# A mixture-of-experts tail: where the third shared-expert batch is computed

## The chip, the cores and the metric

The kernel runs on one NeuronCore of a Trainium2 chip. The metric is the device time of one launch in microseconds (us). TensorE is called PE, VectorE DVE, ScalarE ACT, GpSimd POOL and SyncE SP, as the profile does.

## What is computed

Four batches of 512 tokens, each token a row of 256 numbers, go through two layers, all in float32:

```python
x = x + xattn(layernorm(x), ctx)              # 16 heads, causal mask
xf = layernorm(x).reshape(2048, 256)
comb = top-2 softmax weights over 8 experts, from xf @ gate_w.T
for e in range(8):                            # HALF = 384
    y = silu(xf @ wg[e].T) * (xf @ wu[e].T) @ w_down[e].T
    out += comb[:, e:e+1] * y
shared = silu(xf @ sg_gate.T) * (xf @ sg_up.T) @ sg_down.T
x = x + shared + out
```

The change touches only the second layer: the shared expert, which every token passes, and its place beside the eight routed experts.

## The kernel before

**Order.** Every engine has its own instruction list, written out by hand, and the lists meet at semaphores. There is no planner; what stands first on an engine's list runs first. After attention come the second layernorm, the router (a chain of small DVE instructions), the lists of tokens by expert (`token_of`, semaphore `lists_ready`), and then 39 expert tiles of 128 token slots each (`NT` = 39).

**Shared expert.** It runs by batch `b` of 512 tokens, B = 4 batches, with M = 3 pieces `m` of the hidden width. `shared_up(b)` on PE makes gate and up values of a piece in PSUM `set_a`; `shared_silu(b, m)` on ACT and `shared_h(b, m)` on DVE turn them into `sg[:, m]`; `shared_down(b)` on PE multiplies by the down weights into `set_b`, banks 2 and 3; `shared_y(b)` on DVE adds that to the residual rows `x_res`. The last batch is added by two instructions of its own at the very end (L1596). `s_h` counts the `shared_h` that are done, `s_yfree` the batches whose down result has left PSUM (it starts at 1). In the kernel before, batches 0, 1 and 2 run before the expert tiles, in the time of the router and the weight splits, and batch 3 runs after them.

**Weight splits.** The expert up-weights (`wup`) are split into a high and a low part in 8 pieces (`SPLITS`): ACT copies a piece to `wup_hi` (`hi_parts`, L986), DVE writes `wup_lo` = `wup` - `wup_hi` (`lo_part`, L1478). `up_lo` counts the finished low pieces; PE waits for all 8 before the first expert tile. The first four high pieces (`EARLY` = 4) are made before the lists are known.

**Expert tiles.** POOL gathers the rows of a tile from DRAM (`rows_in_tile`, L576). PE transposes them (`rows_t`, L901), ACT and DVE split the result (L986, L1505), PE runs `up` (12 matmuls, L914 to L916), ACT and DVE make the hidden values, PE transposes these (L924) and runs `down` (L933 to L935), DVE weights the result (L1531), and POOL adds the rows to one of two sums in DRAM with an indirect DMA (`add_rows`, L584). The tiles are software pipelined, one tile to a slot.

**End.** When all tiles of a sum are added, SP loads the sum back by four DMAs of 512 tokens (L455, first sum 1, then sum 0), DVE adds them to `x_res` (`add_sum`, L1583; four adds of 128x1024 for sum 1, eight of 128x512 for sum 0), and ACT's queue stores each eighth of `x_res` (L1200). In the kernel before, `shared_h(3, m)` stands on DVE's list in turn with the adds of sum 1.

Of the kernel before, what the change touches and what calls it, by code (L numbers as in the profile page):

```python
# [41 lines left out]
DMA = 16  # L42


def build(nc, x, ctxT, wqT, bq, wkT, bk, wvT, bv, woT, bo, gwT, wupT, wdnT, sgT, suT, sdT, out):
    B, S, D = x.shape
# [6 lines left out]
    QT = S // P  # L53
# [4 lines left out]
    M = HALF // P  # L58
    TOP_K = 2
    NT = (TOP_K * N + E * (P - 1)) // P  # L60
# [19 lines left out]
    with ExitStack() as ctx:  # L80
# [3 lines left out]
        def sem(name):  # L84
            return ctx.enter_context(nc.semaphore(name))
# [129 lines left out]
        def te():  # L215
# [56 lines left out]
        s_up, s_sg, s_h, s_y, s_yfree = (sem(n) for n in ("s_up", "s_sg", "s_h", "s_y", "s_yfree"))  # L272
# [5 lines left out]
        y_in = [[sem(f"y_in{i}_{c}") for c in range(B)] for i in range(2)]  # L278
# [3 lines left out]
        e_xt, e_xTr, e_up, e_sgr, e_hr, e_ht, e_hTr, e_yf, e_yr = (sem(n) for n in  # L282
            ("e_xt", "e_xTr", "e_up", "e_sgr", "e_hr", "e_ht", "e_hTr", "e_yf", "e_yr"))
# [59 lines left out]
        SPLITS = 8  # L343
        EARLY = 4

        def piece(w, i):
            cut = C * E * 2 * HALF // SPLITS
            return w[:].rearrange("p c n -> p (c n)")[:, i * cut:(i + 1) * cut]
# [250 lines left out]
        def _(pe):  # L599
# [235 lines left out]
            def shared_up(b, lo=0, hi=M):  # L835
                for m in range(lo, hi):
                    n = b * M + m
                    if n > 1:
                        pe.wait_ge(s_h, n - 1)
                    for w, dst in zip((wsg, wsu), gu[n % 2]):  # L840
                        for c in range(C):
                            last = mm(dst, w[:, c, m * P:(m + 1) * P], xn2T[:, c, bass.ds(b * S, S)],  # L842
                                      start=c == 0, stop=c == C - 1)
                    last.then_inc(s_up, 1)

            def shared_down(b):
                pe.wait_ge(s_yfree, b + 1)
                for m in range(M):
                    pe.wait_ge(s_h, b * M + m + 1)
                    for j in range(QT):  # L850

                        last = mm(Bk[:, 2 + j // 2, (j % 2) * D:(j % 2 + 1) * D], sg[:, m, j * P:(j + 1) * P],  # L852
                                  wsd[:, m, :], start=m == 0 and j % 2 == 0, stop=m == M - 1,
                                  skip_group_check=True)
                last.then_inc(s_y, 1)
# [34 lines left out]
                          at_tile[:, j, :, :].rearrange("p c t -> p (c t)"), start=j == 0, stop=j == NJ - 1)  # L890
            last.then_inc(hot_full, 1)
            shared_down(1)
            shared_up(2, 0, 2)


            def rows_t(t, a, x, filled, first=False):
                pe.wait_ge(e_in[x], DMA * filled)
                if not first:
                    pe.wait_ge(e_xTr, t)
                for c in range(C):  # L900
                    last = tr(Bk[:, 0, c * P:(c + 1) * P], e_x[:, x, c * P:(c + 1) * P], ident[:])  # L901
                last.then_inc(e_xt, 1)
# [4 lines left out]
            def up(t, a, e):  # L907
                pe.wait_ge(e_xTr, t + 1)
                for i in range(2):
                    for c in range(C):  # L910
                        cols = bass.ds(e * (2 * HALF) + i * HALF, HALF)
                        dst = A[:, 2 * a + i, 0:HALF]

                        mm(dst, e_xT_hi[:, a, c, :], wup_hi[:, c, cols], start=c == 0, stop=False)  # L914
                        mm(dst, e_xT_hi[:, a, c, :], wup_lo[:, c, cols], start=False, stop=False)  # L915
                        last = mm(dst, e_xT_lo[:, a, c, :], wup_hi[:, c, cols], start=False, stop=c == C - 1)  # L916
                last.then_inc(e_up, 1)

            def hidden_t(t, a, first=False):
                pe.wait_ge(e_hr, t + 1)  # L920
                if not first:
                    pe.wait_ge(e_hTr, t)
                for m in range(M):
                    last = tr(Bk[:, 1, m * P:(m + 1) * P], e_h[:, a, m * P:(m + 1) * P], ident[:])  # L924
                last.then_inc(e_ht, 1)

            def down(t, a, e):
                pe.wait_ge(e_hTr, t + 1)
                pe.wait_ge(e_yr, t + 1)
                cols = bass.ds(e * D, D)  # L930
                dst = Bk[:, 2, 0:D]
                for m in range(M):
                    mm(dst, e_hT_hi[:, a, m, :], wdn_hi[:, m, cols], start=m == 0, stop=False)  # L933
                    mm(dst, e_hT_hi[:, a, m, :], wdn_lo[:, m, cols], start=False, stop=False)  # L934
                    last = mm(dst, e_hT_lo[:, a, m, :], wdn_hi[:, m, cols], start=False, stop=m == M - 1)  # L935
                last.then_inc(e_yf, 1)
# [1 line left out]

            pe.wait_ge(hot_read, 1)
            rows_t(0, 0, 0, 1, True)  # L940
            shared_up(2, 2, 3)
            rows_t(1, 1, 1, 1)
            shared_down(2)
            pe.wait_ge(experts_known, 1)
            first = [expert(t) for t in range(3)]
            pe.wait_ge(up_lo, SPLITS)
            pe.wait_ge(s_h, (B - 1) * M)
            up(0, 0, first[0])
            rows_t(2, 0, 2, 1)
            up(1, 1, first[1])  # L950
            rows_t(3, 1, 3, 1)
            pe.wait_ge(s_yfree, B)
            hidden_t(0, 0, True)
            up(2, 0, first[2])

# [21 lines left out]
            down(NT - 2, (NT - 2) % 2, e_last[1])  # L977
            down(NT - 1, (NT - 1) % 2, e_last[2])
            pe.wait_ge(e_hr, NT)
            shared_up(3)  # L980
            pe.wait_ge(e_yr, NT + 1)
            shared_down(3)

        @block.scalar
        def _(act):
# [147 lines left out]
            def shared_silu(b, m):  # L1133
                act.wait_ge(s_up, b * M + m + 1)
                nc.scalar.activation(sg[:, m, :], gate[(b * M + m) % 2], ACT.Silu).then_inc(s_sg, 1)

            def hi_parts(pieces):
                for i in pieces:
                    copy(piece(wup_hi, i), piece(wup, i)).then_inc(up_hi, 1)
# [6 lines left out]
                shared_silu(1, m)  # L1146
            act.wait_ge(lists_ready, 1)
            act.wait_ge(who_stored, DMA)
            hi_parts(range(EARLY, EARLY + 1))
            shared_silu(2, 0)  # L1150
            hi_parts(range(EARLY + 1, EARLY + 2))
            shared_silu(2, 1)
            hi_parts(range(EARLY + 2, SPLITS))

            def rows_t(t, a):
                act.wait_ge(e_xt, t + 1)
                copy(e_xT_hi[:, a], Bk[:, 0, 0:C * P].rearrange("p (c n) -> p c n", c=C)
                     ).then_inc(e_xhi, 1)
# [7 lines left out]
                copy(e_hT_hi[:, a], Bk[:, 1, 0:M * P].rearrange("p (c n) -> p c n", c=M)).then_inc(e_hThi, 1)  # L1166

            rows_t(0, 0)
            shared_silu(2, 2)
            rows_t(1, 1)  # L1170
            silu(0, 0)
            rows_t(2, 0)
# [15 lines left out]
            silu(NT - 1, (NT - 1) % 2)  # L1188
            hidden_t(NT - 2, (NT - 2) % 2)
            hidden_t(NT - 1, (NT - 1) % 2)  # L1190
            for m in range(M):
                shared_silu(3, m)
            o_t = out.rearrange("b (k p) d -> p (b k) d", p=P)
            for c in range(2 * B):
                if c // 2 < B - 1:
# [7 lines left out]
        def _(dve):  # L1203
# [188 lines left out]
            def shared_h(b, m):  # L1392
                dve.wait_ge(s_sg, b * M + m + 1)
                up_ = (A[:, 1, :], A[:, 3, :])[(b * M + m) % 2]
                v.tensor_tensor(sg[:, m, :], up_, sg[:, m, :], ALU.mult).then_inc(s_h, 1)

            def shared_y(b):
                dve.wait_ge(s_y, b + 1)
                rows = xs_all[:, bass.ds(b * QT, QT), :]
                v.tensor_tensor(rows, Bk[:, 2:4, :].rearrange("p a (k d) -> p (a k) d", k=2), rows,  # L1400
                                ALU.add).then_inc(s_yfree, 1)
# [74 lines left out]
            def lo_part(i):  # L1476
                dve.wait_ge(up_hi, i + 1)
                v.tensor_tensor(piece(wup_lo, i), piece(wup, i), piece(wup_hi, i), ALU.subtract).then_inc(up_lo, 1)  # L1478
# [13 lines left out]
            v.tensor_reduce(tok, lists, AX.X, ALU.add).then_inc(hot_read, 1)  # L1492
            dve.wait_ge(hot_read, 1)
            v.tensor_scalar(token_of[:], tok, io_np, None, ALU.add).then_inc(lists_ready, 1)  # L1494
            shared_y(1)

            lo_part(2)
            shared_h(2, 0)
            lo_part(3)
            lo_part(EARLY)  # L1500
            shared_h(2, 1)

            def rows_lo(t, a):
                dve.wait_ge(e_xhi, t + 1)
# [33 lines left out]
            lo_part(EARLY + 1)  # L1538
            rows_lo(0, 0)
            lo_part(EARLY + 2)  # L1540
            shared_h(2, 2)
            rows_lo(1, 1)
            lo_part(EARLY + 3)
            weights(0, 0, True)
            weights(1, 1, True)
            shared_y(2)
            hidden(0, 0)
            rows_lo(2, 0)
            weights(2, 2)
# [31 lines left out]
            def add_sum(i, at, ready):  # L1581
                dve.wait_ge(*ready)
                v.tensor_tensor(xs_all[:, at, :], xs_all[:, at, :], y_sum[i][:, at, :], ALU.add).then_inc(y_added, 1)  # L1583

            for m in range(M):
                shared_h(3, m)
                add_sum(1, slice(m * QT, (m + 1) * QT), (y_in[1][m], DMA))
            add_sum(1, slice(T - QT, T), (y_in[1][B - 1], DMA))
            for c in range(2 * B):
                dve.wait_ge(y_added, c // 2 + 1)  # L1590
                add_sum(0, slice(2 * c, 2 * c + 2), (y_in[0][c // 2], DMA))
# [43 lines left out]
```

## Time and profile before

| what | value |
|---|---|
| median of 3 runs | 506.07 us (505.5 to 507.34) |
| the profiled execution's own time | 505.84 us |
| its span in the profile | 504.1 us |
| mean granted TensorE clock | 0.977 |
| PE busy | 455.0 us, 90% |
| DVE, ACT, POOL busy | 309.2, 210.1, 193.2 us |
| HBM traffic | 81 GB/s over the span |

The span runs from the first to the last instruction of the profiled execution; its own time is 1.74 us longer. A busy PE is not a PE at its peak, since the ends of matmuls are modelled. Busy shares are averages over stages that are limited by different things, so the rows further down are taken stage by stage. The granted clock is a share of 2.4 GHz; 0.5 is the lower level, 1.2 GHz.

### The profile page before, as it was taken

To read this page: it belongs to the slowest core of one execution; us is meant where nothing else is said; L and a number is where in the kernel's file an instruction comes from. 1 tells how busy PE (TensorE), PEld (TensorE's weight loads), DVE (VectorE), ACT (ScalarE), POOL (GpSimd) and SP (SyncE) were. 2 spreads that over 40 slices of the span, in tenths; PEclk is the share of its full clock that TensorE was granted. 3 is DMA by queue.
4 is the path that set the end of the run, shared out by engine and by line. 5 is a ranking of instruction groups with operands and counts; after the bars stand their busy time and mean duration, and the time that the engine had idled before them with its cause. 6 is when DMAs were issued, how large, how long until landed. Compare 5 with 4: busy or idle time off the path is not lost.

```text
span 504.1 us, 10169 instructions
## 1 busy us (share of the span) xinstructions
PE 455.0 (90%) x3098; PEld 316.2 (63%) x3099; DVE 309.2 (61%) x651; ACT 210.1 (42%) x419; POOL 193.2 (38%) x204
## 2 busy tenths in 40 slices
PE   7668999999999999997769799999999999999993
PEld 6444444464446544473346356499999999999852
DVE  4975656647574766546865596865455455455437
ACT  1235566616665275716773452522332232332210
POOL 4130346305451145401332001226666666666420
PEclk9976999999999999999999999999999999999997
DMA  8934121231124221220098910113444434434379
GB/s 273 255 83 127 38 90 40 96 126 63 66 73 135 73 74 53 89 90 3 4 358 285 416 38 11 32 33 54 73 64 73 74 63 72 75 63 70 37 193 337
DMA packets 45574, 53.84 MB, mean 107 GB/s; under 512 B 7760, under 2 KB 41872, under 8 KB 44912
## 3 DMA queue, kind: packets, MB, share of 16 engines
q1 hardware_dynamic: 34320, 39.77, 24.1%
q0 software_dynamic: 7488, 10.31, 12.6%
q10 hardware_dynamic: 3744, 3.47, 2.4%
q8 instruction: 13, 0.21, 0.2%
q14 instruction: 9, 0.07, 0.1%
HBM read 27.09 MB, written 13.67 MB: 81 GB/s over the span
## 4 chain that ended last, share of the span: by engine, by line
PE 66%; ACT 11%; DVE 11%; DMA 6%; issue 5%; SPq 1%; DVEq 0%; ACTq 0%; POOLq 0%
PE set_a L618 7%; ACT attention L1063 6%; PE set_b L648 6%; PE set_a L915 5%; PE set_a L916 5%; PE set_a L914 5%; PE set_a L669 4%; PE set_a L842 4%; PE set_b L638 4%; DVE attention L1293 3%; PE set_b L933 3%; PE set_a L823 3%; PE set_b L935 3%; PE set_b L934 3%; PE set_b L852 2%
## 5 line engine op out<-in xcount | busy, mean ns | idle before, releaser
L1293 DVE TENSOR_REDUCE attention<-set_a 128x2 f32<-128x1024 f32 (+2 forms) x96 | 96.0, 1041 | 32.3 <-PE set_a L620 30.3
L1063 ACT ACTIVATE attention<-set_b 128x512 f32<-128x512 f32 (+1 forms) x176 | 88.5, 570 | 60.4 <-PE set_b L638 47.8
L525 POOL TENSOR_SCALAR_AFFINE_SELECT attention<-attention 128x512 f32<-128x512 f32 x64 | 40.9, 652 | 120.4 <-ACT attention L1063 120.4
L584 POOL DMA_INDIRECT sum_rows<-moe,token_of x39 | 61.8, 1585 | 43.8 <-issue 29.6
L638 PE MATMUL set_b<-attention 99*128 99x512 bf16 (+3 forms) x256 | 59.9, 307 | 12.2 <-ACT attention L1063 9.7
L618 PE MATMUL set_a<-attention 96*128 96x512 bf16 (+3 forms) x256 | 63.9, 315 | 5.2 <-DVE attention L1293 3.6
L576 POOL DMA_INDIRECT e_x<-normed_rows,token_of x39 | 39.4, 1011 | 62.9 <-DVE token_of L1494 36.5
L1162 ACT ACTIVATE moe<-set_a 128x384 f32<-128x384 f32 x39 | 19.2, 492 | 105.0 <-PE set_a L916 105.0
L1519 DVE TENSOR_TENSOR moe<-set_a,moe 128x384 f32<-128x384 f32 x39 | 21.8, 558 | 62.8 <-ACT moe L1162 61.2
L618 PEld LDWEIGHTS set_a<-attention 96*128 96x128 bf16 x256 | 25.7, 101 | 47.3 <-DVE attention L1293 16.8
L914 PE MATMUL set_a<-wup_hi,e_xT_hi 128*128 x156 | 53.0, 340 | 0.0
L915 PE MATMUL set_a<-wup_lo,e_xT_hi 128*128 x156 | 52.8, 339 | 0.0
L916 PE MATMUL set_a<-wup_hi,e_xT_lo 128*128 x156 | 52.8, 338 | 0.0
L620 PE MATMUL set_a<-maskb,identb 128*128 128x128 bf16 x256 | 50.6, 226 | 0.0
L648 PE MATMUL set_b<-attention 128*32 128x128 f32 (+3 forms) x512 | 43.8, 441 | 1.3 <-ACT attention L986 1.2
L638 PEld LDWEIGHTS set_b<-attention 99*128 99x128 bf16 x256 | 19.3, 98 | 35.1 <-ACT attention L1063 24.4
L933 PE MATMUL set_b<-w_down_hi,e_hT_hi 128*128 x117 | 36.4, 311 | 1.1 <-DVE moe L1531 0.8
L986 ACT ACTIVATE attention<-set_b 12x512 bf16<-12x512 f32 (+4 forms) x48 | 25.8, 597 | 22.8 <-PE set_b L811 10.2
L986 ACT ACTIVATE attention<-attention 128x512 bf16<-128x512 f32 x32 | 19.6, 645 | 32.0 <-DVE attention L1243 28.9
L935 PE MATMUL set_b<-w_down_hi,e_hT_lo 128*128 x117 | 32.9, 281 | 0.0
L934 PE MATMUL set_b<-w_down_lo,e_hT_hi 128*128 x117 | 32.9, 281 | 0.0
L506 POOL TENSOR_TENSOR attention<-attention 128x512 f32<-128x512 f32 x14 | 15.9, 1155 | 43.2 <-ACT attention L986 43.2
(166 smaller groups left out, 837.7 us busy)
## 6 DMA issues: line engine op xcount, KB each, us to landing
attention<-attention SPq DMA_DIRECT2D x182, 64.0 KB, 2.6
wup<-in_wupT SPq DMA_DIRECT2D x2, 3072.0 KB, 14.2
sum_rows<-attention SPq DMA_DIRECT2D x2, 2048.0 KB, 12.8
wup<-sum_rows SPq DMA_DIRECT2D x8, 512.0 KB, 7.0
attention<-in_ctxT SPq DMA_DIRECT2D x7, 512.0 KB, 6.0
w_down<-in_wdnT SPq DMA_DIRECT2D x3, 1024.0 KB, 5.1
x_res<-in_x SPq DMA_DIRECT2D x4, 512.0 KB, 6.9
out<-x_res ACTq DMA_DIRECT2D x8, 256.0 KB, 4.0
```

Source lines behind the costliest of these rows:

```text
L584: g.indirect_dma_start(acc[i], bass.IndirectOffsetOnAxis(token_of[:, t:t + 1], 0), e_y[:, t % 2, :], None, compute_op=ALU.add).then_inc(ad ...
L618: mm(dst, qstack[0:ROWS, g // 2, h, k * P:w], kstack[0:ROWS, g // 2, h, 0:w], start=True, stop=False)
L620: last = mm(dst[:, k * P:w], identb[:], maskb[:], start=False, stop=True)
L638: last = mm(bank(par)[:, i * w:(i + 1) * w], kstack[0:ROWS + 3, g // 2, h, k * P:(k + 1) * P], qstack[0:ROWS + 3, g // 2, h, k * P:S], sta ...
L648: last = mm(pv_bank[32 * h:32 * h + 32, k * P:S], vaug[:, k, HG * g + h, :], pT[k][:, h, :], start=k == 0, stop=k == QT - 1, tile_position ...
L914: mm(dst, e_xT_hi[:, a, c, :], wup_hi[:, c, cols], start=c == 0, stop=False)
L915: mm(dst, e_xT_hi[:, a, c, :], wup_lo[:, c, cols], start=False, stop=False)
L916: last = mm(dst, e_xT_lo[:, a, c, :], wup_hi[:, c, cols], start=False, stop=c == C - 1)
L933: mm(dst, e_hT_hi[:, a, m, :], wdn_hi[:, m, cols], start=m == 0, stop=False)
L934: mm(dst, e_hT_hi[:, a, m, :], wdn_lo[:, m, cols], start=False, stop=False)
L1063: nc.scalar.activation(pT[k][:, h:h + heads, :], bank(par)[:, 0:heads * (S - k * P)], ACT.Exp).then_inc(b_free, 1)
L1293: v.tensor_reduce(dst, src, AX.X, ALU.max, negate=True).then_inc(a_free, 1)
```

## The change

On PE, `shared_up(2)` and `shared_down(2)` leave the place ahead of the expert tiles and stand between the last tile's `down` and `shared_up(3)`. The wait for the last tile's result (`e_yr`) moves from ahead of `shared_down(3)` to ahead of `shared_down(2)`. Two waits ahead of the tiles count one batch less (`s_h`, `s_yfree`).

On ACT, `hi_parts` of pieces 4 to 7 run in one go after the lists; `shared_silu(2, m)` stand ahead of `shared_silu(3, m)` at the end. On DVE, `lo_part(2)` stands ahead of `shared_y(1)` instead of behind it, the three `shared_h(2, m)` and `shared_y(2)` leave the stretch ahead of the tiles, and the end is written in a new order: all `shared_h(2, m)`, two adds of sum 1, `shared_y(2)`, then `shared_h(3, m)` in turn with the other two adds of sum 1, and behind them the eight adds of sum 0. No DMA is added or taken away, and no instruction but the waits changes in number.

```diff
--- before.py
+++ after.py
@@ -890,7 +890,6 @@
                           at_tile[:, j, :, :].rearrange("p c t -> p (c t)"), start=j == 0, stop=j == NJ - 1)
             last.then_inc(hot_full, 1)
             shared_down(1)
-            shared_up(2, 0, 2)
 
 
             def rows_t(t, a, x, filled, first=False):
@@ -938,18 +937,16 @@
 
             pe.wait_ge(hot_read, 1)
             rows_t(0, 0, 0, 1, True)
-            shared_up(2, 2, 3)
             rows_t(1, 1, 1, 1)
-            shared_down(2)
             pe.wait_ge(experts_known, 1)
             first = [expert(t) for t in range(3)]
             pe.wait_ge(up_lo, SPLITS)
-            pe.wait_ge(s_h, (B - 1) * M)
+            pe.wait_ge(s_h, (B - 2) * M)
             up(0, 0, first[0])
             rows_t(2, 0, 2, 1)
             up(1, 1, first[1])
             rows_t(3, 1, 3, 1)
-            pe.wait_ge(s_yfree, B)
+            pe.wait_ge(s_yfree, B - 1)
             hidden_t(0, 0, True)
             up(2, 0, first[2])
 
@@ -977,8 +974,10 @@
             down(NT - 2, (NT - 2) % 2, e_last[1])
             down(NT - 1, (NT - 1) % 2, e_last[2])
             pe.wait_ge(e_hr, NT)
+            shared_up(2)
+            pe.wait_ge(e_yr, NT + 1)
+            shared_down(2)
             shared_up(3)
-            pe.wait_ge(e_yr, NT + 1)
             shared_down(3)
 
         @block.scalar
@@ -1146,11 +1145,7 @@
                 shared_silu(1, m)
             act.wait_ge(lists_ready, 1)
             act.wait_ge(who_stored, DMA)
-            hi_parts(range(EARLY, EARLY + 1))
-            shared_silu(2, 0)
-            hi_parts(range(EARLY + 1, EARLY + 2))
-            shared_silu(2, 1)
-            hi_parts(range(EARLY + 2, SPLITS))
+            hi_parts(range(EARLY, SPLITS))
 
             def rows_t(t, a):
                 act.wait_ge(e_xt, t + 1)
@@ -1166,7 +1161,6 @@
                 copy(e_hT_hi[:, a], Bk[:, 1, 0:M * P].rearrange("p (c n) -> p c n", c=M)).then_inc(e_hThi, 1)
 
             rows_t(0, 0)
-            shared_silu(2, 2)
             rows_t(1, 1)
             silu(0, 0)
             rows_t(2, 0)
@@ -1188,8 +1182,9 @@
             silu(NT - 1, (NT - 1) % 2)
             hidden_t(NT - 2, (NT - 2) % 2)
             hidden_t(NT - 1, (NT - 1) % 2)
-            for m in range(M):
-                shared_silu(3, m)
+            for b in range(B - 2, B):
+                for m in range(M):
+                    shared_silu(b, m)
             o_t = out.rearrange("b (k p) d -> p (b k) d", p=P)
             for c in range(2 * B):
                 if c // 2 < B - 1:
@@ -1492,13 +1487,10 @@
             v.tensor_reduce(tok, lists, AX.X, ALU.add).then_inc(hot_read, 1)
             dve.wait_ge(hot_read, 1)
             v.tensor_scalar(token_of[:], tok, io_np, None, ALU.add).then_inc(lists_ready, 1)
+            lo_part(2)
             shared_y(1)
-
-            lo_part(2)
-            shared_h(2, 0)
             lo_part(3)
             lo_part(EARLY)
-            shared_h(2, 1)
 
             def rows_lo(t, a):
                 dve.wait_ge(e_xhi, t + 1)
@@ -1538,12 +1530,10 @@
             lo_part(EARLY + 1)
             rows_lo(0, 0)
             lo_part(EARLY + 2)
-            shared_h(2, 2)
             rows_lo(1, 1)
             lo_part(EARLY + 3)
             weights(0, 0, True)
             weights(1, 1, True)
-            shared_y(2)
             hidden(0, 0)
             rows_lo(2, 0)
             weights(2, 2)
@@ -1583,9 +1573,16 @@
                 v.tensor_tensor(xs_all[:, at, :], xs_all[:, at, :], y_sum[i][:, at, :], ALU.add).then_inc(y_added, 1)
 
             for m in range(M):
-                shared_h(3, m)
-                add_sum(1, slice(m * QT, (m + 1) * QT), (y_in[1][m], DMA))
+                shared_h(2, m)
+            for b in range(B - 2):
+                add_sum(1, slice(b * QT, (b + 1) * QT), (y_in[1][b], DMA))
+            shared_y(2)
+            shared_h(3, 0)
+            dve.wait_ge(s_yfree, B)
+            add_sum(1, slice(2 * QT, 3 * QT), (y_in[1][2], DMA))
+            shared_h(3, 1)
             add_sum(1, slice(T - QT, T), (y_in[1][B - 1], DMA))
+            shared_h(3, 2)
             for c in range(2 * B):
                 dve.wait_ge(y_added, c // 2 + 1)
                 add_sum(0, slice(2 * c, 2 * c + 2), (y_in[0][c // 2], DMA))
```

## Rows read from the trace of the kernel before

**Rows 1.** The chain that ended last, 474 to 504 us: start, length, what.

```profile
482.11 5.79 DMA sum_rows<-moe,token_of
...
489.43 8.93 DMA wup<-sum_rows
...
499.66 0.68 DVE x_res L1596
```

**Rows 2.** Timeline of the end, 469 to 504 us: start, length, engine, line, instruction.

```profile
479.93 1.88 PE L842 MATMUL set_a<-moe,w_sg 128*128 128x512 f32 x4
...
490.23 5.34 PE L852 MATMUL set_b<-w_sd,moe 128*128 128x256 f32 x24
...
491.06 0.69 DVE L1395 TENSOR_TENSOR moe<-set_a,moe 128x512 f32<-128x512 f32 x1 [0.44 <-ACT moe L1135]
491.66 3.61 DVE L1583 TENSOR_TENSOR x_res<-x_res,wup 128x1024 f32<-128x1024 f32 x4
...
498.45 1.29 DVE L1583 TENSOR_TENSOR x_res<-x_res,wup 128x512 f32<-128x512 f32 x2 [0.16 <-DMA wup<-sum_rows]
```

**Rows 3.** One stretch of the tile loop: length, each engine's busy time, clock, DMA.

```profile
404.00:408.00 4.00, 4.00 (x31) 3.96 (x30) 2.30 (x8) 1.36 (x4) 2.55 (x3) 1.00 0.39 66
```

**Rows 4.** Timeline up to the first tile, 308 to 333 us.

```profile
308.89 5.42 PE L852 MATMUL set_b<-w_sd,moe 128*128 128x256 f32 x24
...
311.36 1.48 ACT L986 ACTIVATE wup_hi<-wup 128x1536 fp32r<-128x1536 f32 x1 [2.85 <-DVE token_of L1494]
...
314.15 1.88 PE L842 MATMUL set_a<-moe,w_sg 128*128 128x512 f32 x4
314.35 1.23 DVE L1400 TENSOR_TENSOR x_res<-set_b,x_res 128x1024 f32<-128x1024 f32 x1 [3.02 <-PE set_b L852]
...
315.49 1.75 DVE L1478 TENSOR_TENSOR wup_lo<-wup,wup_hi 128x1536 fp32r<-128x1536 f32 x1
...
316.26 1.81 POOL L576 DMA_INDIRECT e_x<-normed_rows,token_of  x1 [0.30 <-issue]
...
319.02 3.41 DVE L1478 TENSOR_TENSOR wup_lo<-wup,wup_hi 128x1536 fp32r<-128x1536 f32 x2
...
324.86 0.42 DVE L1505 TENSOR_TENSOR e_xT_lo<-set_b,e_xT_hi 128x256 fp32r<-128x256 f32 x1 [0.16 <-ACT e_xT_hi L986]
...
327.80 1.75 DVE L1478 TENSOR_TENSOR wup_lo<-wup,wup_hi 128x1536 fp32r<-128x1536 f32 x1
...
330.67 0.53 PE L914 MATMUL set_a<-wup_hi,e_xT_hi 128*128 x1
...
332.98 0.38 PE L901 MATMUL set_b<-ident,e_x 128*128 128x128 f32 x2
```

**Rows 5.** The line of the gathers: its instructions, and issue to landing.

```profile
L576 POOL DMA_INDIRECT e_x<-normed_rows,token_of x39: 951/989/1807, 312.3 to 461.2; - x39
...
DMA to landing us min/median/max: 2.7/2.8/3.3
```

**Rows 6.** Timeline of PE early in the span.

```profile
24.20 1.94 PE L606 MATMUL set_b<-ident,attention 128*128 128x128 f32 x8 [4.26 <-DVE attention L1231]
...
39.95 0.58 PE L618 MATMUL set_a<-attention 96*128 96x512 bf16 x1 [1.42 <-ACT attention L986]
...
43.74 0.53 PE L618 MATMUL set_a<-attention 96*128 96x384 bf16 x1
44.06 0.31 PE L620 MATMUL set_a<-maskb,identb 128*128 128x128 bf16 x1
```

**Rows 7.** Half-microsecond stretches: busy by engine, granted clock (1.00 is full), DMA.

```profile
24.00:24.50 0.50, 0.30 (x2) 0.34 (x3) 0.50 (x3) 0.00 (x0) 0.00 (x0) 0.50 1.11 92
27.00:27.50 0.50, 0.50 (x5) 0.23 (x4) 0.25 (x1) 0.20 (x1) 0.00 (x0) 0.60 0.97 96
47.50:48.00 0.50, 0.50 (x8) 0.50 (x7) 0.27 (x1) 0.50 (x2) 0.00 (x0) 0.62 0.68 231
498.00:498.50 0.50, 0.00 (x0) 0.00 (x0) 0.34 (x2) 0.00 (x0) 0.00 (x0) 0.94 1.11 389
```

## Prediction, made before the changed kernel was run

> **What bounds the kernel now.** I read three stages. First the end: in the chain of waits the last work goes from the last indirect add of tile rows (482.11, 5.79 us) through SP's issue to the loads of the sums (from 489.43, 8.93 us), to DVE's final adds at 499.66 and the last store [rows 1]. The shared expert is not in that chain. In the timeline PE starts `shared_up(3)` at 479.93, goes on to `shared_down(3)` at 490.23 and is through at 490.23 + 5.34 = 495.57, while the add that needs it starts at 499.66 [rows 1, 2]: PE has 4.1 us to spare there.
>
> Second the tiles: in a stretch of the loop PE is busy 4.00 of 4.00 us at granted clock 1.00, with DVE at 2.30 and POOL at 2.55 [rows 3]. The loop goes at PE's pace, so a tile phase that starts earlier ends earlier by the same amount.
>
> Third the stretch ahead of the tiles: PE starts `shared_up(2)` at 314.15 and `up(0)` at 330.67 [rows 4]. DVE's last `lo_part` starts at 327.80 and ends at 329.55, 1.1 us before `up(0)`. So PE, with the shared work, sets the start of the tiles, but only by 1.1 us; DVE's splits are right behind.
>
> **The change, part by part.** What leaves the front of PE's list is 24 matmuls of `shared_up` and 24 of `shared_down`. The first take 490.23 - 479.93 = 10.30 us, the second 314.15 - 308.89 = 5.26 us from start to the next start [rows 2, 4]: 15.56 us in all. All of it comes back at the end. PE's total work is unchanged; what counts is where PE becomes idle.
>
> *Front.* With that work gone `up(0)` waits for `up_lo` = 8, so for DVE. DVE's new order: `lo_part(2)` at once after the lists (its input is ready since the first four high pieces are early), from about 311.36 to 313.11, in a stretch in which DVE waits for the down result of batch 1; that is free. `shared_y(1)` starts at 314.35 as before, since it follows `shared_down(1)`, which hasn't moved. From there: 1.14 us to the next start (315.49 - 314.35), five low pieces at 1.66 us each (two take 3.41, so a start follows a start by 3.41 - 1.75) = 8.30, two `rows_lo` at 0.34 (0.42 less the same overlap) = 0.68, and 0.09 for the last piece's full length [rows 4]. 314.35 + 10.21 = 324.56, and with 0.09 us of signalling `up(0)` starts at 324.65. Its other inputs hide: ACT's pieces 4 to 7 take four times at most 1.48 from 311.36, to 317.3; its copy of tile 0's rows follows at once, and DVE asks for that only at 320.5. The transposes of tile 1 stand between two DVE steps and have the 1.66 us of `lo_part(6)` to hide in. The tile phase could so start 330.67 - 324.65 = **6.0 us** earlier.
>
> The gathers are covered too. They are issued from 312.26 on and land 2.7 to 3.3 us later [rows 5], so tile 0 is in at about 315.4, five microseconds before its `rows_lo`. The fourth took 1.81 us beside a `lo_part`, the median is 0.99 [rows 4, 5]; the moved `lo_part(2)` now lies beside the first one. If that costs the same 0.8 us, it still hides; without the cover it would cost 0.8 us. The Trainium skill (page "SBUF — State Buffer", on its shared port pair) says that a GpSimd operation and a DVE operation with two SBUF inputs can block each other through a port that they share. The 1.81 us agrees with it; by it the start of the tiles would not move either.
>
> *Clock.* The price is PE's idle time. After 314.15 PE has only the transposes of two tiles until 324.65. After an idle stretch of 4.26 us [rows 6] the clock was down to 0.50 at 24.0 to 24.5, and it was down again within 3 us of PE's last matmul at 495.57 (0.94 in the half microsecond from 498.0) [rows 7]. So `up(0)` starts at the lower level. How long it lasts shows at two places: work from 24.20 saw the clock rise in the stretch from 27.0 (0.60, so near 27.4), 3.2 us; patchier work from 39.95 saw it rise in that from 47.5 (0.62, near 47.9), 7.9 us [rows 6, 7]. At full clock the 12 matmuls of `up(0)` take 332.98 - 330.67 = 2.31 us, 0.19 each [rows 4]; at the lower level a 384-column matmul takes 44.06 - 43.74 = 0.32 us [rows 6]. The share lost is 1 - 0.19/0.32 = 0.4, so 1.3 us for 3.2 and 3.2 us for 7.9. I take 1.5, near the first, since the tile work is as gapless as that from 24.20. The tile phase is then **4.5 us** earlier at its end (between 2.8 and 6.0).
>
> The Trainium skill (page "TensorE: Matmul & The Clock Gate", Part 1) says that the throttled state is the default which only activity releases, and that the penalty is half of the throttled time. By that rule it would be 1.6 instead of 1.5 us, and the sum 0.1 us more.
>
> *End.* In the time of the profile before, less the 4.5: PE runs `shared_up(2)`, `shared_down(2)`, `shared_up(3)` from 479.93. None of them waits: `sg[:, 2]` of batch 2 is ready at 491.06 + 0.69 = 491.75, and `shared_down(2)` asks for it 3.5 us after its start at 490.23. So the ups are through at 479.93 + 10.30 + 5.26 + 10.30 = 505.79. In the profile before, the same point is 490.23, `shared_h(3, 2)` started 0.83 us and the next add 1.43 us behind it [rows 2]. Now DVE's list has all eight adds of sum 0 *behind* `shared_h(3, 2)`, at 0.605 us from start to start (499.66 - 498.45 for two) [rows 1, 2]: 505.79 + 1.43 + 8 x 0.605 = 512.06 for the start of the final add. PE's `shared_down(3)` ends at 505.79 + 5.34 = 511.13, 0.9 us earlier, so the order on DVE decides. The loads of the sums ended near 498.4 [rows 1], long before, so the DMA chain that set the end is off the path. From the start of the final add to the end of the span the two adds and the last store take 504.1 - 499.66 = 4.44 us. The stores no longer share the engines with loads, but now follow each other at 0.605 us; I keep 4.44, with 0.5 less as the lower bound (an estimate: a store that meets no queue).
>
> Sum: 512.06 - 4.5 + 4.44 = 512.0, that is 7.9 us over the span of 504.1. The steps: 6.0 gained ahead of the tiles, 1.5 lost to the clock, 15.56 added at the end, of which 4.1 fill PE's spare time, and 0.9 for the adds behind DVE's last product: -6.0 + 1.5 + 15.56 - 4.1 + 0.9 = 7.9. The profiled execution's own time was 505.84 (the median is 506.07, 0.2 more), so I predict **513.8 us**.
>
> **Rivals.**
> *The clock lasts longer* (7.9 us at the lower level, as from 39.95): 3.2 instead of 1.5, 515.5 us. For it: the short transposes ahead; against it: PE has no gaps after 324.65. *The clock costs nothing* (the transposes of tiles 0 and 1 hold it up): 512.3 us. Against it: some 5 us lie between them.
>
> *The end hides the batch, and the kernel is faster.* If the chain of adds, loads and stores still set the end, the whole tile phase's gain would be kept: 505.84 - 4.5 = 501.3 us. Its place is PE's list behind the tiles; it decides if the added work is no more than the spare 4.1 us plus what the chain gives. The rows speak against it: 15.56 us of matmuls at full clock, on one engine, in order, against 4.1. About 11.5 us of it would have to vanish; to break even, 11.5 + 0.9 - 4.5 = 7.9 us would.
>
> *No gain ahead of the tiles.* Something else holds `up(0)` near 330.67, such as gathers that wait behind DVE or ACT's pieces; then 4.5 is missing, 518.3 us. Against it: the gathers have 5 us of cover and the pieces 3.
>
> *PE, not DVE, sets the end* (the adds of sum 0 go faster than 0.605): 0.9 us less, 512.9.
>
> **How the numbers follow.** The forecast, 512.9 case included, has 0.70; the longer clock 0.12; the free clock 0.09; no gain in front 0.04; the hidden batch 0.03; another cause of no change 0.02. The range is 511.8 (free clock and 0.5 off the last store) to 516.3 (the longer clock and 0.5 for the scatter of runs): it holds the first three cases, with some taken off for terms that are off together. About 0.5%, 2.5 us, is what a measurement of this kernel can tell from no change. Faster 0.03, same 0.02, slower 0.95.
>
> **What would show it.** Right: `up(0)` near 324.7 with the granted clock at 0.50 for the first 3 to 4 us; about 10 us with little PE work ahead of it; PE's last `down` 4.5 us earlier; `shared_down(3)` ending near 506.6; the final adds starting near 507.6, right behind eight adds of sum 0; the chain of waits running over PE's shared matmuls in place of the loads. Wrong: `up(0)` released by ACT or a gather; a clock of 1.00 throughout; a tile slot in the loop whose length changes, which would multiply by 39; or PE waiting between `shared_up(2)` and `shared_down(3)`.

## The result, and the profile after

The changed kernel takes 514.84 us (median of 4 runs, 513.13 to 517.67), the kernel before 506.7 (4 runs, 505.5 to 507.39). The ratio is 1.0169 with a 95% interval of 1.0116 to 1.0221: it is slower by 1.2 to 2.2%. The profiled execution took 514.28 us. A ratio, here and below, is worked out from all runs of a set and can differ from the quotient of the two medians by some tenths of a per cent.

The page of the profile after, its span, its busy times and the granted clock in 40 slices:

```profile
span 512.5 us, 10170 instructions
...
PE 461.9 (90%) x3098; PEld 320.1 (62%) x3099; DVE 307.4 (60%) x651; ACT 210.1 (41%) x419; POOL 194.8 (38%) x204
...
PEclk9965999999999999999989999699999999999999
```

The span is 8.4 us longer than before. Cut at four marks that both profiles have, it comes apart as follows: `token_of` (the end of the lists) starts at 311.08 before and 312.25 after; `up(0)` at 330.67 and 325.89; the first shared matmul behind the tiles at 479.93 and 476.42; the final add at 499.66 and 508.45; the end is at 504.1 and 512.5.

| stretch | before | after | difference | forecast |
|---|---|---|---|---|
| start to `token_of` | 311.08 | 312.25 | +1.17 | 0 |
| `token_of` to `up(0)` | 19.59 | 13.64 | -5.95 | -6.0 |
| tiles: `up(0)` to the first shared matmul behind | 149.26 | 150.53 | +1.27 | +1.5 |
| shared matmuls to the final add | 19.73 | 32.03 | +12.30 | +12.4 |
| final add to the end | 4.44 | 4.05 | -0.39 | 0, at least -0.5 |
| span | 504.1 | 512.5 | +8.4 | +7.9 |

The forecast for the fourth stretch is 512.06 - 479.93 less the 19.73 of before.

The timeline ahead of the tiles, after (start, length, engine, line; compare [rows 4]):

```profile
312.41 1.75 DVE L1473 TENSOR_TENSOR wup_lo<-wup,wup_hi 128x1536 fp32r<-128x1536 f32 x1
312.53 5.61 ACT L985 ACTIVATE wup_hi<-wup 128x1536 fp32r<-128x1536 f32 x4 [2.85 <-DVE token_of L1489]
313.43 1.75 POOL L576 DMA_INDIRECT e_x<-normed_rows,token_of  x1 [36.48 <-DVE token_of L1489]
...
315.52 1.23 DVE L1395 TENSOR_TENSOR x_res<-set_b,x_res 128x1024 f32<-128x1024 f32 x1 [1.35 <-PE set_b L852]
316.66 5.09 DVE L1473 TENSOR_TENSOR wup_lo<-wup,wup_hi 128x1536 fp32r<-128x1536 f32 x3
316.76 2.47 POOL L576 DMA_INDIRECT e_x<-normed_rows,token_of  x1 [0.30 <-issue]
...
317.10 0.41 PE L900 MATMUL set_b<-ident,e_x 128*128 128x128 f32 x2 [1.62 <-DMA e_x<-normed_rows,token_of]
...
321.66 0.42 DVE L1497 TENSOR_TENSOR e_xT_lo<-set_b,e_xT_hi 128x256 fp32r<-128x256 f32 x1
...
323.99 1.75 DVE L1473 TENSOR_TENSOR wup_lo<-wup,wup_hi 128x1536 fp32r<-128x1536 f32 x1
...
325.89 0.68 PE L913 MATMUL set_a<-wup_hi,e_xT_hi 128*128 x1 [3.01 <-DVE wup_lo L1473]
```

`lo_part(2)` at 312.41 fills DVE's wait, DVE goes through its pieces without a gap from 315.52, and the row of `up(0)` names its releaser: DVE's `wup_lo`, not PE's own list. PE only waits between 317.51 and 322.23, and again, after the transposes of tile 1, for the 3.01 us ahead of `up(0)`. The first and the third gather take 1.75 and 2.47 us.

The granted clock there, in stretches of 1 us (the clock is the third number from the end of a row; compare [rows 7]):

```profile
317.00:318.00 1.00, 0.41 (x2) 0.20 (x2) 1.00 (x1) 1.00 (x1) 1.00 (x1) 1.00 0.49 133
...
319.00:320.00 1.00, 0.00 (x0) 0.00 (x0) 1.00 (x2) 0.00 (x0) 0.69 (x2) 0.50 0.11 29
325.00:326.00 1.00, 0.11 (x1) 0.11 (x1) 0.96 (x4) 0.00 (x0) 0.00 (x0) 0.50 0.00 0
328.00:329.00 1.00, 1.00 (x5) 1.00 (x4) 0.00 (x0) 0.00 (x0) 0.89 (x1) 0.50 0.43 104
329.00:330.00 1.00, 1.00 (x8) 0.97 (x7) 0.00 (x0) 0.28 (x1) 0.07 (x1) 0.96 0.32 79
```

The clock is still full at 317, half from 319 on, and rises again just after 329 (0.96 over that stretch, so near 329.08): from the start of `up(0)` at 325.89 PE runs 3.2 us at the lower level.

The end, after (compare [rows 2]):

```profile
476.42 1.88 PE L842 MATMUL set_a<-moe,w_sg 128*128 128x512 f32 x4
...
486.72 5.34 PE L852 MATMUL set_b<-w_sd,moe 128*128 128x256 f32 x24
...
491.90 1.88 PE L842 MATMUL set_a<-moe,w_sg 128*128 128x512 f32 x4
...
502.20 5.34 PE L852 MATMUL set_b<-w_sd,moe 128*128 128x256 f32 x24
...
503.03 0.69 DVE L1390 TENSOR_TENSOR moe<-set_a,moe 128x512 f32<-128x512 f32 x1 [1.61 <-ACT moe L1134]
503.63 4.89 DVE L1573 TENSOR_TENSOR x_res<-x_res,wup 128x512 f32<-128x512 f32 x8
...
508.45 1.28 DVE L1593 TENSOR_TENSOR x_res<-set_b,x_res 128x512 f32<-128x512 f32 x2
```

And the chain of waits there, whose rows of before were the indirect adds and the loads of the sums [rows 1]:

```profile
476.58 10.30 PE set_a L842 x24
486.88 5.18 PE set_b L852 x24
492.06 10.31 PE set_a L842 x24
...
504.23 3.76 DVE x_res L1573 x7
...
508.45 0.69 DVE x_res L1593
```

PE's 24, 24 and 24 matmuls of two ups and a down stand in it in one piece, 25.8 us, and then DVE's adds of sum 0. The loads of the sums have left the chain. The last product starts at 503.03, the eight adds behind it take 503.63 to 508.52, and the final add starts at 508.45, though PE's last matmul ended at 502.20 + 5.34 = 507.54: the adds, not PE, are last, by 0.9 us.

### The profile page after: what moved, and what is told of

Same layout as the page of the kernel before. It is cut to its first block, busy times and chain, and to the rows that moved or that the text cites. A ratio compares the mean times of both kernels' runs of the same rounds, so it can differ in the third digit from the quotient of the medians.

```text
span 512.5 us, 10170 instructions
## 1 busy us (share of the span) xinstructions
PE 461.9 (90%) x3098; PEld 320.1 (62%) x3099; DVE 307.4 (60%) x651; ACT 210.1 (41%) x419; POOL 194.8 (38%) x204
## 4 chain that ended last, share of the span: by engine, by line
PE 69%; DVE 12%; ACT 9%; issue 5%; DMA 3%; SPq 1%; DVEq 0%; ACTq 0%
PE set_a L618 7%; PE set_a L842 6%; PE set_b L648 6%; PE set_a L913 6%; PE set_a L914 5%; PE set_a L915 5%; ACT attention L1062 5%; PE set_a L669 4%; PE set_b L638 4%; PE set_b L932 3%; PE set_a L823 3%; PE set_b L933 3%; PE set_b L934 3%; DVE attention L1288 3%; PE set_b L923 2%
## 5 line engine op out<-in xcount | busy, mean ns | idle before, releaser
L638 PE MATMUL set_b<-attention 99*128 99x512 bf16 (+3 forms) x256 | 61.2, 314 | 11.9 <-ACT attention L1062 9.9
L618 PE MATMUL set_a<-attention 96*128 96x512 bf16 (+3 forms) x256 | 65.0, 320 | 5.2 <-DVE attention L1288 3.1
L576 POOL DMA_INDIRECT e_x<-normed_rows,token_of x39 | 41.1, 1053 | 56.6 <-DVE token_of L1489 36.5
L648 PE MATMUL set_b<-attention 128*32 128x128 f32 (+3 forms) x512 | 45.4, 455 | 0.4 <-ACT attention L985 0.3
```

The lines of the kernel that those rows point to most:

```text
L618: mm(dst, qstack[0:ROWS, g // 2, h, k * P:w], kstack[0:ROWS, g // 2, h, 0:w], start=True, stop=False)
L638: last = mm(bank(par)[:, i * w:(i + 1) * w], kstack[0:ROWS + 3, g // 2, h, k * P:(k + 1) * P], qstack[0:ROWS + 3, g // 2, h, k * P:S], sta ...
L648: last = mm(pv_bank[32 * h:32 * h + 32, k * P:S], vaug[:, k, HG * g + h, :], pT[k][:, h, :], start=k == 0, stop=k == QT - 1, tile_position ...
```

## The experiments

Medians are of sets that were run with the kernel before on the same chip; its own median was 506.49 in the first set (e1 to e4), 506.54 in the second (e5 to e8) and 506.73 in the third (e9 to e11).

### e1: hold the clock

```diff
+            pe.wait_ge(s_h, (B - 2) * M)
...
+            def keep_busy(count):
+                for _ in range(count):
+                    mm(A[:, 2, :], wsg[:, 0, 0:P], xn2T[:, 0, 2 * S:3 * S], start=True, stop=True)
...
             rows_t(0, 0, 0, 1, True)
+            keep_busy(5)
             rows_t(1, 1, 1, 1)
+            keep_busy(3)
```

The added wait lets batch 1's products finish first, since the calls write a bank that held its gate values. The eight calls are sixteen matmuls in the trace, ten and six.

> The changed kernel with eight extra 512-column matmuls into an unused PSUM bank while PE waits for DVE's splits (five behind the transposes of tile 0, three behind those of tile 1); nothing reads their result. If the clock is the price that the prediction puts at 1.5 us (1.3 in the changed kernel's trace), up(0) starts at the same point, the granted clock is 1.00 over the tiles, and the time is 1.3 us less than the changed kernel's, near 513.5. If the clock costs nothing, or the rest of the loss lies there, the time stays at 514.8 or drops by several us.

Measured: 511.6 us (511.2 to 511.82), ratio 1.008 (1.0056 to 1.0104). `up(0)` starts 13.64 us behind `token_of`, as in the changed kernel, the granted clock is 1.00 from there on, and the tiles take 149.45 us. That the clock is a price is shown; but 3.2 us below the changed kernel is more than the 1.3 expected, so the size of the price is taken up again in e8, e9 and e11.

### e2: part of the adds of sum 0 ahead of the last product

```diff
             add_sum(1, slice(T - QT, T), (y_in[1][B - 1], DMA))
...
+            add_sum0(range(0, 4))
             shared_h(3, 2)
-            for c in range(2 * B):
+            add_sum0(range(4, 2 * B))
```

(`add_sum0(cs)` is the loop over `c` of the changed kernel, for the given `c`.)

> The changed kernel with the first four of the eight adds of sum 0 placed ahead of DVE's last shared-expert product instead of behind it. If the adds behind that product decide the end by 0.9 us, the final add now waits for PE and starts 0.9 us earlier, and the last store goes out with less ahead of it: 0.9 to 1.4 us less, near 513.7. If PE or the stores decide anyway, no change (514.8).

Measured: 513.76 us (513.3 to 514.71), ratio 1.0127 (1.01 to 1.0153). The medians alone (1.1 us apart, with intervals that overlap) don't settle it; the stretch does. From the first shared matmul behind the tiles to the final add it is 31.16 us instead of 32.03. The end of its timeline:

```profile
500.57 3.62 DVE L1573 TENSOR_TENSOR x_res<-x_res,wup 128x1024 f32<-128x1024 f32 x5
...
504.71 2.49 DVE L1573 TENSOR_TENSOR x_res<-x_res,wup 128x512 f32<-128x512 f32 x4
507.94 1.29 DVE L1598 TENSOR_TENSOR x_res<-set_b,x_res 128x512 f32<-128x512 f32 x2 [0.75 <-PE set_b L852]
```

The row of five adds is one of sum 1 and four of sum 0, ahead of the product; four are left behind it, and the final add now waits 0.75 us for PE. So in the profile DVE's order decided the end by 0.9 us, as the prediction had it.

### e3: lo_part(2) back behind shared_y(1)

```diff
-            lo_part(2)
             shared_y(1)
+            lo_part(2)
             lo_part(3)
```

> The changed kernel with lo_part(2) back behind shared_y(1) on DVE. If DVE's list of splits alone sets the start of the tiles, up(0) starts 1.7 us later and the whole kernel ends 1.7 us later, near 516.5. If a gather or ACT's copies hold the tiles, the time stays at 514.8. The first gather should take about 1 us instead of 1.75, since no split lies beside it.

Measured: 516.73 us (514.74 to 516.83), ratio 1.0183 (1.0159 to 1.0206). `token_of` to `up(0)` is 15.31 us instead of 13.64: 1.67 us, one piece, arrives at the tiles in full. DVE's list sets their start. The gathers of this kernel, on POOL:

```profile
311.89 1.15 POOL L576 DMA_INDIRECT e_x<-normed_rows,token_of  x1 [36.49 <-DVE token_of L1489]
313.35 0.97 POOL L576 DMA_INDIRECT e_x<-normed_rows,token_of  x1 [0.31 <-issue]
314.62 0.95 POOL L576 DMA_INDIRECT e_x<-normed_rows,token_of  x1 [0.30 <-issue]
315.88 1.80 POOL L576 DMA_INDIRECT e_x<-normed_rows,token_of  x1 [0.30 <-issue]
```

and DVE's pieces beside them:

```profile
315.11 6.76 DVE L1473 TENSOR_TENSOR wup_lo<-wup,wup_hi 128x1536 fp32r<-128x1536 f32 x4
```

The first gather takes 1.15 us with no split beside it, 1.75 in the changed kernel, where `lo_part(2)` lies beside it; the third 0.95 against 2.47. DVE's pieces stay at 1.75 us, so it is the gather that gives way. The start times say when: a gather that starts while a piece is running ends 0.8 to 1.0 us behind the end of that piece (fourth gather here: the piece ends at 315.11 + 1.75 = 316.86, the gather at 317.68; in the changed kernel the third: 318.41 and 319.23), and the next piece does not hold it. The third gather here was under way when the first piece started, and neither is longer for it. The Trainium skill (page "SBUF — State Buffer", on its shared port pair) has this as a port that GpSimd and a DVE operation with two SBUF inputs share; the trace agrees with a gather that waits, and shows no cost for the tiles.

### e4 and e5: without batch 2

e4 takes the batch out of every list and numbers batch 3 as the third; the rows of batch 2 lack their shared expert. The part of its edit on PE's list:

```diff
-            shared_up(2)
-            pe.wait_ge(e_yr, NT + 1)
-            shared_down(2)
             shared_up(3)
+            pe.wait_ge(e_yr, NT + 1)
             shared_down(3)
```

> The changed kernel without the shared expert's batch 2: its up, silu, product, down and add are left out everywhere, so those rows lack it. If PE's list behind the tiles sets the end, the end falls back on the chain of adds, loads and stores: the gain in front of 4.7 us is all kept, and the time is near 502, some 13 us under the changed kernel and 4 to 5 under the kernel before. If the chain hides the batch (the rival that ends faster), leaving it out changes nothing: 514.8.

Measured: 505.91 us (504.37 to 507.4), ratio 0.998 (0.9952 to 1.0008), so neither what I expected (502) nor what the rival did (514.8). Its timeline behind the tiles:

```profile
483.94 1.22 DVE L1571 TENSOR_TENSOR x_res<-x_res,wup 128x1024 f32<-128x1024 f32 x1 [6.15 <-DMA wup<-sum_rows]
485.42 1.23 DVE L1571 TENSOR_TENSOR x_res<-x_res,wup 128x1024 f32<-128x1024 f32 x1 [0.26 <-DMA wup<-sum_rows]
486.56 0.68 DVE L1388 TENSOR_TENSOR moe<-set_a,moe 128x512 f32<-128x512 f32 x1
...
487.30 3.78 PE L842 MATMUL set_a<-moe,w_sg 128*128 128x512 f32 x4 [3.94 <-DVE moe L1388]
...
490.87 3.09 PE L842 MATMUL set_a<-moe,w_su 128*128 128x512 f32 x4
```

Taking `shared_h(2, m)` out had left the products of batch 3 behind two adds of sum 1 on DVE, and these wait for loads (6.15 us of idle ahead of the first). The first product of batch 3 so came only at 486.56, PE stood 3.94 us for it and then ran at the lower clock (four matmuls in 3.78 us instead of the 1.88 of [rows 2]). The stretch from the first shared matmul to the final add is 23.72 us. My experiment had brought a new wait with it. e5 takes it out (its edit against e4):

```diff
-            for b in range(B - 2):
-                add_sum(1, slice(b * QT, (b + 1) * QT), (y_in[1][b], DMA))
-            shared_h(2, 0)
-            add_sum(1, slice(2 * QT, 3 * QT), (y_in[1][2], DMA))
-            shared_h(2, 1)
-            add_sum(1, slice(T - QT, T), (y_in[1][B - 1], DMA))
-            shared_h(2, 2)
+            for m in range(M):
+                shared_h(2, m)
+                add_sum(1, slice(m * QT, (m + 1) * QT), (y_in[1][m], DMA))
+            add_sum(1, slice(T - QT, T), (y_in[1][B - 1], DMA))
```

> The changed kernel without batch 2 of the shared expert (its rows lack it), and with DVE's products of batch 3 again in turn with the adds of sum 1, as in the kernel before. In e4 the first product stood behind two adds that wait for loads, PE stood 3.9 us for it and then ran at the lower clock. If that order was what e4 added, the end is again the chain of adds, loads and stores, and the time is 4 to 5 us below the kernel before, near 502. If something else holds the end, it stays near 506.

Measured: 503.2 us (502.06 to 503.77), ratio 0.992 (0.9889 to 0.9952), and in the chain of waits the transfers are back:

```profile
479.50 5.01 DMA sum_rows<-moe,token_of
...
486.78 8.95 DMA wup<-sum_rows
...
497.03 0.68 DVE x_res L1584
```

The stretch from the first shared matmul to the final add is 19.73 us, to the hundredth that of the kernel before. The 12.3 us of the changed kernel are therefore batch 2's work on PE with the adds behind it. That 503.2 is 1 us above the expected 502 goes with the tiles, 152.04 us in its profile against 150.53; more on this at e8.

### e6: the new order of the splits alone

```diff
+            lo_part(2)
             shared_y(1)
-            lo_part(2)
-            shared_h(2, 0)
             lo_part(3)
             lo_part(EARLY)
+            shared_h(2, 0)
             shared_h(2, 1)
```

(and `hi_parts(range(EARLY, SPLITS))` in one go on ACT.)

> The kernel before with only the new order of the splits: ACT's pieces 4 to 7 in one go, DVE's lo_part(2) ahead of shared_y(1); batch 2 stays ahead of the tiles. If PE's shared work sets the start of the tiles, nothing changes (506.5). If DVE's or ACT's list sets it, up(0) starts up to 1.1 us earlier or 1 us later.

Measured: 505.61 us (504.55 to 507.28), ratio 0.9971 (0.995 to 0.9992). `token_of` to `up(0)` is 18.83 us, 0.8 less than before, though I had expected none. By itself the part of the change that isn't a move of work gives a little: 0.1 to 0.5%. The traces show where the 0.8 us lay. The transposes of tile 1, in the kernel before and then here:

```profile
325.43 0.41 PE L901 MATMUL set_b<-ident,e_x 128*128 128x128 f32 x2 [0.60 <-DVE e_xT_lo L1505]
```

```profile
325.17 0.41 PE L901 MATMUL set_b<-ident,e_x 128*128 128x128 f32 x2
```

In the kernel before they start 4.20 us behind the last piece of `shared_up(2)` (at 321.23), because ACT copied two high pieces ahead of tile 0's rows and DVE's `rows_lo` came late; here they start 3.44 us behind it (at 321.73) and wait for nobody. So PE's list had a wait in it ahead of the tiles, and of the 5.95 us that the changed kernel gains there 0.76 are the new order's and 5.2 the moved work's.

### e7: only the down matmuls go behind the tiles

```diff
+        sg_held = (xn2T[:, 1, 0:S], xn2T[:, 1, S:2 * S], xn2T[:, 0, S:2 * S])
...
             shared_down(1)
-            shared_up(2, 0, 2)
+            shared_up(2, 0, 1)
...
             rows_t(0, 0, 0, 1, True)
-            shared_up(2, 2, 3)
+            shared_up(2, 1, 2)
             rows_t(1, 1, 1, 1)
-            shared_down(2)
+            shared_up(2, 2, 3)
...
             shared_up(3)
+            shared_down(2)
             pe.wait_ge(e_yr, NT + 1)
             shared_down(3)
```

The moved `shared_down(2)` writes banks 0 and 1 of `set_b`. On DVE the products of batch 2 stand between the splits, and `shared_y(2)` between the fourth and the fifth add of sum 0. `lo_part(2)` and ACT's pieces stand as in e6.

> A version of my own on the kernel before: batch 2's up, silu and product stay ahead of the tiles, where they fill PE's wait for the splits and hold the clock; only its down matmuls (5.3 us) go behind the tiles, into the two other banks, with the product held in dead columns of the transposed rows. If the account is right, up(0) starts about 3.9 us earlier with the clock at 1.00, PE is through 5.2 us later behind the tiles of which 4.1 are spare, and the time is 2.5 to 3 us below the kernel before, near 503.6. If PE's idle time ahead of the tiles is of no matter, it is 5.2 - 4.1 = 1.1 us above, near 507.6.

Measured: 502.63 us (501.07 to 503.63), ratio 0.9906 (0.9876 to 0.9936): faster than both kernels. The timeline at the start of the tiles and the chain at the end:

```profile
324.08 1.75 DVE L1483 TENSOR_TENSOR wup_lo<-wup,wup_hi 128x1536 fp32r<-128x1536 f32 x1
...
325.77 0.69 DVE L1399 TENSOR_TENSOR moe<-set_a,moe 128x512 f32<-128x512 f32 x1
...
326.68 0.44 PE L919 MATMUL set_a<-wup_hi,e_xT_hi 128*128 x1 [1.57 <-DVE wup_lo L1483]
```

```profile
476.41 10.30 PE set_a L846 x24
486.71 10.38 PE set_b L857 x48
...
497.11 0.69 DVE x_res L1602
```

`up(0)` starts 15.54 us behind `token_of`, 4.05 less than before (3.9 expected). The tiles take 149.57 us at clock 1.00, where the changed kernel took 150.5 and more. The final add starts 20.86 us behind the first shared matmul, 1.13 more than before (1.1 expected), released by PE. The medians are 3.9 us apart, the spans 2.9 (504.1 and 501.2), against 2.5 to 3 expected. PE's wait for the splits is mostly filled (1.57 us are left) by work that must be done somewhere; what went to the end, 5.2 us, is a little more than PE's spare time there, and 1.1 us of it was paid. A part of the gain is e6's order: against e6 (505.61 us, same set) e7 is 3.0 us faster.

### e8 to e11: how large the clock's share is

e8 and e11 are the changed kernel, e9 is e1, e10 is e1 with e2's order.

> The changed kernel once more, as the yardstick of this set: 514.8, and by the same chip against the kernel before 1.017. If e1 was low only because its early stretches ran luckier, this one may be as low as 513.

> e1 once more, beside the changed kernel in the same set, since e1 came out 3.2 us under it where 1.3 was forecast. By the stretches of the profiles so far, the tiles take 149.5 us with the clock held and 150.5 to 152.0 without, so 1.0 to 2.5 us is the clock's, and the rest of e1's 3.2 was the early part of the span, which ran 0.5 to 1.5 us short. Then this one is 1.0 to 2.5 us under the changed kernel here. If the extra matmuls give more than the clock, it is 3 us again, with the tiles at 149.5.

> e1 and e2 together: the clock held and four adds of sum 0 ahead of the last product. If the two are independent, the time is 0.9 us under e9, with the stretch from the first shared matmul behind the tiles to the final add at 31.16 us as in e2.

> The changed kernel as the yardstick of this set, 514.8 to 515.2; tiles between 150.5 and 152.0 us.

| kernel | median us | ratio (95%) | tiles in its profile, us |
|---|---|---|---|
| e8, changed | 515.21 | 1.0146 (1.0102 to 1.019) | 151.94 |
| e11, changed | 514.08 | 1.0141 (1.0118 to 1.0165) | 151.84 |
| e9, clock held | 512.56 | 1.0104 (1.008 to 1.0128) | 149.45 |
| e10, clock held, sum 0 first | 511.75 | 1.0103 (1.0079 to 1.0128) | 149.42 |

Why the same kernel's tiles take 150.53 us in one profile and 151.94 in another shows in e8's granted clock, in stretches of 1 us:

```profile
325.00:326.00 1.00, 0.89 (x3) 0.89 (x4) 0.53 (x4) 0.00 (x0) 0.00 (x0) 0.50 0.00 0
329.00:330.00 1.00, 1.00 (x5) 0.90 (x5) 0.13 (x1) 0.65 (x2) 0.00 (x0) 0.50 0.39 112
330.00:331.00 1.00, 1.00 (x6) 1.00 (x5) 0.97 (x4) 0.16 (x1) 0.00 (x0) 0.65 0.00 0
331.00:332.00 1.00, 1.00 (x7) 1.00 (x6) 0.08 (x1) 0.00 (x0) 0.13 (x1) 1.00 0.00 0
```

`up(0)` started at 325.11 and the clock rose near 330.7 (0.65 over that stretch): 5.6 us at the lower level instead of 3.2. In the seven profiles without work on PE ahead of the tiles it was 3.0 to 3.2 us three times (the changed kernel, e2, e3), 4.4 once (e4) and 5.6 to 5.7 three times (e5, e8, e11). `up(0)` to the first shared matmul is 149.26 to 149.57 us in every profile where PE had work up to the tiles (before, e1, e6, e7, e9, e10) and 150.53 to 152.04 in every one where it had none (the changed kernel three times, e2 to e5): 1.0 to 2.8 us for the clock. In the set of e9 and e11 the medians are 1.5 us apart, inside that. e1's 3.2 us did not come back. The rest of it would be an early part that ran short by chance; that fits e1's `token_of` (310.67 against 312.25 in the changed kernel) but isn't proven by one profile. e10's stretch behind the tiles is 31.15 us against 32.03, as in e2. Its median is 0.8 us under e9's, but the two ratios are the same (1.0103 and 1.0104), so the whole time doesn't confirm the 0.9 us; the stretch does. One of the four executions of e8 took 512.04 us at a mean clock of 0.977, where the other three had 0.959; no trace of it was kept, but the numbers are those of the kernels with the clock held.

## Why the prediction was right, step by step

- *PE sets the start of the tiles, DVE is right behind.* Right. `up(0)` came 5.95 us nearer to the lists (6.0 forecast), released by DVE's last low piece; e3 moved it by one piece. What the prediction left out is that PE's list in the kernel before had a wait of its own for ACT and DVE (0.60 us ahead of the transposes of tile 1); without it 5.2 us would have been there to gain, not 6.0 (e6). The sum didn't suffer, since it went by DVE's list.
- *The gathers are covered.* Right in what mattered: the first took the 0.8 us more that the prediction allowed for (1.75), the third more than that (2.47), and tile 0's rows were still there over 4 us before DVE wanted them.
- *The clock costs 1.5 us, between 1.3 and 3.2.* Right in kind, the bounds held, the value was somewhat low. The changed kernel's profile gives 1.27 us over before and the other profiles 1.6 to 2.8 (150.90 to 152.04 less 149.26). The forecast took the short of two stretches as the likely one because tile work is gapless; with such work the time at the lower level still came out between 3.0 and 5.7. That the value fell near the forecast in the first profile is in part luck. The share lost was low too: it came from 0.19 us a matmul, which is 2.31 us over 12 with a slower first one; the matmuls after it start every 0.176 us, which against 0.32 is 0.45 instead of 0.4, and e8's 5.6 us cost 2.5 against e9's tiles, 0.45 as well. The rival with a free clock is refuted by the granted clock of 0.50 and by e1 and e9; that of a clock that stays low for 7.9 us did not occur in a profile.
- *The loop goes at PE's pace.* Right: the tiles' length changed by no more than the clock, so nothing multiplied by 39.
- *15.56 us are added, 4.1 of them in PE's spare time, and 0.9 for adds behind the last product.* Right: 12.30 against 12.4. e5 shows the 12.3 as a whole, e2 the 0.9 alone, e7 the 4.1 (5.2 us added, 1.13 paid).
- *The last add and store take 4.44, perhaps 0.5 less.* The lower bound was nearer: 4.05 in the changed kernel and 4.01 to 4.11 wherever the last stores met no loads; 4.44 to 4.47 where the loads of the sums had just ended (before, e5, e6).
- *The rival that ends faster.* Its mechanism is real, and e5 shows it with the batch left out: where PE's list is short enough, transfers set the end and the gain in front is kept (503.2). It did not apply, since 15.56 us don't fit into 4.1.
- The span was forecast 7.9 us longer and is 8.4: 1.17 of that arose ahead of `token_of`, where neither kernel differs, and the other terms are 0.7 below the forecast. The two partly cancel in the span, which is luck. Such differences in the early part (`token_of` between 310.67 and 312.25 over the profiles) are part of each kernel's scatter. The upper end of the range does not follow from its own terms (515.5 + 0.5 is 516.0, not 516.3); nothing rests on it.

## What to carry to other kernels

Before work is moved off a list that bounds a stage, find what the engine will do in its place. Here it waited, over 9 us in all, and the same work came back at the end, where it had only 4.1 us to hide in; the gain in front could never exceed the distance to the next bound, which one list of DVE durations gave to 0.1 us. The better split is by size: leave in the gap what fills it, and move about as much as the far end has spare time for (e7, 0.9% faster, and e6's order alone 0.3%, where the whole move was 1.7% slower). When a leave-out experiment misses, look first for a wait that the leaving out itself made, as in e4.

## What the runs showed of the hardware

- A stretch of waiting costs PE twice: after it, the same tiles' first matmuls started every 0.32 us instead of 0.18, for 3.2 us in one execution of the changed kernel and 5.6 in another. This makes the time of the tiles scatter (150.5 to 152.0 us, against 149.3 to 149.6) as well as grow; eight idle-time calls whose result nobody reads took 1.5 us off (e9 against e11).
- Indirect gathers of 0.95 to 1.15 us took 1.36 to 2.47 us where they started while a DVE subtraction of two SBUF operands was running: each ended 0.8 to 1.0 us behind the end of that subtraction, which kept its 1.75 us (changed kernel and e3). A gather that was under way when a subtraction started took its usual 0.95 us (e3).
- With the same two adds and last stores the span ended 4.0 to 4.1 us behind the start of the final add when the loads of the sums were long over, and 4.4 to 4.5 when they had just ended (e4 against e5).
